# Four graph layers on one core: lots in one pair of PSUM banks, sums of propagations kept in three, similarity passes over two chunks

## The reference

```python
h = jnp.maximum(_layernorm(x, axis=-1), 0.0)
# layer 0
Wh = h @ W + b
sim = dot(Wh[row], Wh[col]) / max(|Wh[row]| * |Wh[col]|, 1e-8)
base = adj_v * softplus(deg_coeff[0] * deg_v + deg_coeff[1]) * (row != col)
prop_pos = segment_sum((base * relu(sim))[:, None] * Wh[col], row)
prop_neg = segment_sum((base * -relu(-sim))[:, None] * Wh[col], row)
x = x + scale * (coeff[0] * prop_pos + coeff[1] * prop_neg + coeff[2] * Wh)
# layers 1 to 3: sums over the same edges (counts, relu messages, sigmoid-gated messages)
```

## Time and profile before

| | us |
|---|---|
| median of 3 runs | 1847.92 (1847.14 to 1849.7) |
| the profiled execution, whole | 1844.67 |
| its span, first to last instruction | 1843.0 |
| `build`, blocks (first one-hot to last add) | 329.4 to 1184.2 |
| PE busy | 1153.8 (63%) |
| DVE busy | 1161.9 (63%) |
| ACT busy | 458.6 (25%) |
| mean granted clock of PE | 0.794 |

### The profile page before, as it was taken

The page is one execution under the profiler, slowest core; times in us unless marked ns, Lnnn a source line. Parts: engine busy times, 40 slices in busy tenths (PEclk is TensorE's granted clock), DMA queues, the critical chain, the costliest instruction groups (busy, mean ns, idle before and its releaser), DMA issues. The chain is left out here.

```text
span 1843.0 us, 38373 instructions
## 1 busy us (share of the span) xinstructions
PE 1153.8 (63%) x16508; PEld 977.7 (53%) x16508; DVE 1161.9 (63%) x2153; ACT 458.6 (25%) x1133; POOL 125.3 (7%) x215
## 2 busy tenths in 40 slices
PE   0000231677777877777787777547564767589997
PEld 0000121465655655655565556447564766389997
DVE  4860314888888888888888888659696442422222
ACT  1000101544444444444444444100000000012221
POOL 0710005200000000000000000000000000000000
PEclk9999956777778777777777777569786978579999
DMA  7316012121121121121121211164000000055552
GB/s 181 89 31 46 2 36 56 56 91 73 55 109 55 56 109 55 55 109 55 78 87 55 95 69 55 56 279 168 1 2 1 2 1 3 2 213 198 201 211 89
DMA packets 40247, 146.66 MB, mean 80 GB/s; under 512 B 24156, under 2 KB 24700, under 8 KB 33276
## 3 DMA queue, kind: packets, MB, share of 16 engines
q1 hardware_dynamic: 36252, 135.03, 20.9%
q0 software_dynamic: 2912, 7.92, 1.6%
q10 hardware_dynamic: 896, 1.04, 0.3%
HBM read 80.27 MB, written 63.72 MB: 78 GB/s over the span
## 5 line engine op out<-in xcount | busy, mean ns | idle before, releaser
L1065 PE MATMUL b_ps<-b_u_b,b_y 128*128 128x64 f32 x1250 | 207.8, 317 | 112.1 <-DVE k_xs L1028 106.5
L1065 PEld LDWEIGHTS b_ps<-b_u_b,b_y 128*128 128x128 f32 x1250 | 192.4, 233 | 131.5 <-DVE b_y L1022 128.5
L1232 PE MATMUL gcn_ps<-c_u,c_c 128*128 128x192 bf16 x1875 | 160.6, 250 | 117.2 <-PEq L85 77.3
L1065 PE MATMUL b_ps<-b_mv,b_soh 64*128 64x50 bf16 (+1 forms) x9600 | 221.1, 206 | 18.4 <-DVE b_mv L1006 12.9
L1232 PEld LDWEIGHTS gcn_ps<-c_u,c_c 128*128 128x128 bf16 x1875 | 159.3, 100 | 118.4 <-issue 77.8
L1065 PEld LDWEIGHTS b_ps<-b_mv,b_soh 64*128 64x128 bf16 x9600 | 196.1, 107 | 42.4 <-DVE b_mv L1006 13.9
L927 ACT ACTIVATE b_c_row<-b_ps 128x300 bf16<-128x300 f32 (+1 forms) x275 | 115.4, 420 | 408.6 <-PE b_ps L1065 407.3
L1006 DVE TENSOR_TENSOR b_mv<-b_mv,b_two 128x468 bf16<-128x468 bf16 (+1 forms) x600 | 179.5, 367 | 0.0
L1111 PEld LDWEIGHTS b_ps<-k_ident,b_a_row 128*128 128x128 f32 x625 | 81.3, 165 | 150.9 <-issue 93.6
L1111 PE MATMUL b_ps<-k_ident,b_a_row 128*128 128x128 f32 x625 | 129.5, 335 | 49.4 <-DVE b_scale L1014 49.4
L1014 DVE SCALAR_TENSOR_TENSOR b_scale<-head_rn_row,head_cap,b_ps 128x512 f32<-128x512 f32 (+1 forms) x175 | 120.3, 687 | 60.4 <-PE b_ps L1111 59.7
(11 more groups left out here) (224 smaller groups left out, 1080.7 us busy)
## 6 DMA issues: line engine op xcount, KB each, us to landing
g_blocks<-b_g_row SPq DMA_DIRECT2D x25, 1600.0 KB, 7.5
gated_row<-g_blocks SPq DMA_DIRECT2D x25, 1600.0 KB, 6.9
c_blocks<-b_c_row SPq DMA_DIRECT2D x25, 800.0 KB, 3.3
c_c<-c_blocks SPq DMA_DIRECT2D x5, 4000.0 KB, 32.1
edges_attr<-in_edge_attr SPq DMA_DIRECT2D x1, 5642.0 KB
head_rn_row<-rn SPq DMA_DIRECT2D x1, 1600.0 KB
rec<-sort_rec SPq DMA_DIRECT2D x1, 1209.0 KB, 4.9
k_xs<-in_x SPq DMA_DIRECT2D x1, 768.0 KB
```

Source lines behind the costliest of these rows:

```text
L1065: return nc.tensor.matmul(out, lhsT, rhs, start=start, stop=True, skip_group_check=True)
L1232: return nc.tensor.matmul(out, lhsT, rhs, start=start, stop=True, skip_group_check=True)
```

## The change

The eight PSUM banks are given out anew: lots have banks 0 and 1 alone, the similarities 2 and 3, AT is bank 4, and banks 5 to 7 (`SUM`) keep the propagations of 24 of the 25 column blocks through all 25 steps, with matmuls that add up in the bank. The 25th column block goes to AT[0:64] and is still added by DVE once in a step. The other adds are replaced by three at the very end (`folded`). `pos`, `sim` and `y` are made for two chunks at once (1024 columns, 4 groups `NG` in place of 7 chunks); `scale` and the transposes stay by chunk. The one-hots are split in two parts, "hi" and "hot", and both tables of order are new. A lot now waits for the copies of the lot just before it (`3 * i + 6` in place of `3 * i + 3`). The tiles `rel`, `qt` and `rest` of the head share the memory of `y`, and twelve small matmuls with zeros open the three sum banks.

```diff
-ORDER = [("lot", 0), ("lot", 1), ("chunk", 0), ("lot", 2), ("lot", 3), ("chunk", 1), ("prop", 0), ("lot", 4), ("chunk", 2),
...
+ORDER = [("lot", 0), ("chunk", 0), ("lot", 1), ("chunk", 1), ("lot", 2), ("prop", 0), ("lot", 3), ("prop", 1), ("chunk", 2),
+         ("lot", 4), ("chunk", 3), ("lot", 5), ("prop", 2), ("lot", 6), ("prop", 3), ("chunk", 4), ("lot", 7), ("chunk", 5),
+         ("lot", 8), ("lot", 9), ("chunk", 6), ("prop", 4), ("lot", 10), ("prop", 5), ("prop", 6)]
+VORDER = [("hi", 1), ("hot", 1), ("scale", 0), ("sim", 0), ("scale", 1), ("hi", 2), ("y", 0), ("hot", 2),
+          ("scale", 2), ("sim", 1), ("scale", 3), ("hi", 3), ("y", 1), ("hot", 3),
+          ("scale", 4), ("sim", 2), ("scale", 5), ("hi", 0), ("y", 2), ("scale", 6), ("sim", 3), ("y", 3), ("hot", 0), ("add", 0)]
...
-        SIM, AT, PR = 4, 6, 7
+        SIM, AT, SUM = 2, 4, 5
...
-            def positive(v, i):
...
+            def positive(v, g):
+                act.wait_ge(s["sims"], NG * v + (NG + g + 1))
+                nc.scalar.activation(side(pos, g), both(g), ACT.Relu, scale=coef[:, 0:1]).then_inc(s["pos"], 1)
...
-            def weigh(v, b, i):
...
+            def scaling(v, b, i):
...
+                dve.wait_ge(s["at"], NC * v + (2 * NC + i + 1))
+                nc.vector.scalar_tensor_tensor(scale[g % 2][:, lo:lo + n], rn_row[:, P * h0:P * h0 + n], cap[:, bass.ds(b, 1)],
+                                               ps[:, AT, 0:n], ALU.min, ALU.mult).then_inc(s["scaled"], 1)
+
+            def similar(v, g):
+                dve.wait_ge(s["made"], NG * v + (g + 1))
+                dve.wait_ge(s["pos"], NG * v + (g + 1))
+                nc.vector.scalar_tensor_tensor(side(sim[g % 2], g), both(g), coef[:, 1:2], side(pos, g),
                                                ALU.mult, ALU.add).then_inc(s["sgn"], 1)
...
-            def add(v, i):
-                h0, nh = CHUNKS[i]
-                dve.wait_ge(s["propped"], NC * v + (2 * NC + i + 2))
-                part = prop[:, h0:h0 + nh, :]
-                nc.vector.tensor_tensor(part, part, ps[:, PR, 0:nh * F].rearrange("p (h f) -> p h f", f=F),
-                                        ALU.add).then_inc(s["added"], 1)
...
+            def add(v):
+                dve.wait_ge(s["propped"], NC * v + (3 * NC + 1))
+                nc.vector.tensor_tensor(prop[:, NB - 1, :], prop[:, NB - 1, :], ps[:, AT, 0:F], ALU.add).then_inc(s["added"], 1)
...
+                for q in range(3):
+                    part = prop[:, 8 * q:8 * q + 8, :]
+                    nc.vector.tensor_tensor(part, part, ps[:, SUM + q, :].rearrange("p (h f) -> p h f", f=F), ALU.add).then_inc(s["folded"], 1)
...
+                for q in range(3):
+                    for j in range(4):
+                        mm(ps[:, SUM + q, P * j:P * j + P], k["zeros16"][:, 0:P], k["zeros16"][:, 0:P], j == 0)
...
-                pe.wait_ge(s["evac"], 3 * NL * w + (3 * i + 3))
+                pe.wait_ge(s["evac"], 3 * NL * w + (3 * i + 6))
...
-                            ins = mm(ps[:, 2 * pair + h, to:to + NB * (f1 - f0)], soh[b][rows, at, :], mv[b][rows, at, f0:f1, 0:NB],
+                            ins = mm(ps[:, h, to:to + NB * (f1 - f0)], soh[b][rows, at, :], mv[b][rows, at, f0:f1, 0:NB],
...
-                    pe.wait_ge(s["sgn"], NC * v + (i + 1))
+                    pe.wait_ge(s["sgn"], NG * v + (g + 1))
...
+                    pe.wait_ge(s["added"], v + 1)
                     pe.wait_ge(s["evac"], 3 * NL * v + (3 * NL + 6))
...
-                pe.wait_ge(s["made"], NC * v + (i + 3))
-                pe.wait_ge(s["added"], NC * v + (i + 1))
+                g, lo = i // 2, 512 * (i % 2)
+                pe.wait_ge(s["made"], NG * v + (g + 3))
                 for j in range(nh):
-                    ins = mm(ps[:, PR, F * j:F * j + F], y[i % 2][:, P * j:P * j + P], u_b[par][:, :], True)
+                    h = h0 + j
+                    to = ps[:, SUM + h // 8, h % 8 * F:h % 8 * F + F] if h < NB - 1 else ps[:, AT, 0:F]
+                    ins = mm(to, y[g % 2][:, lo + P * j:lo + P * j + P], u_b[par][:, :], h == NB - 1)
```

More of the change, by code:

```diff
@@ L756, in build @@
         gate_at, zero16, zero = l.sb("gate_at", [P, 1]), l.sb("zero16", [P, 1], BF16), l.sb("zero", [P, 1])
[L757 removed]
+        pos = l.sb("pos", [P, 1024])
         begun = l.sb("begun", [P, 6])
[L759 to L760 removed]
+        sim, scale = [l.sb(f"sim{i}", [P, 1024]) for i in range(2)], [l.sb(f"scale{i}", [P, 1024]) for i in range(2)]
+        y = [l.sb(f"y{i}", [P, 1024]) for i in range(2)]
+        rel, qt, rest = y[0][:, 0:512], y[0][:, 512:1024], y[1][:, :].rearrange("p (a n) -> p a n", a=2)
         ps = l.ps("ps", [P, 8, 512])
         names = ("index turned split rounded doubled hot onehot lot evac sims pos sgn weights made at scaled propped added "
[L763 removed]
+                 "folded further gate")
         s = {n: l.sem(n) for n in names.split()}
@@ L767, in build @@
         block = l.block()
-        SIM, AT, PR = 4, 6, 7
+        SIM, AT, SUM = 2, 4, 5
+        wide = lambda g: P * sum(CHUNKS[i][1] for i in range(2 * g, min(2 * g + 2, NC)))
+        side = lambda tile, g: (tile[:, 0:1024].rearrange("p (a n) -> p a n", a=2) if wide(g) == 1024
+                                else tile[:, 0:wide(g)])
+        both = lambda g: ps[:, SIM:SIM + 2, :] if wide(g) == 1024 else ps[:, SIM, 0:wide(g)]
         again = lambda r: not isinstance(r, int)
@@ L884, in _, with end @@
             pool.wait_ge(s["gate"], 5)
-            plan(pool, head, first, step, lambda r: None, widen)
+            def end(r):
+                if again(r):
+                    add_out(r, NB - 1, 0)
+            plan(pool, head, first, step, end, widen)
         @block.sync
@@ L954, in step @@
                         evacuate(r, w, par, i)
-                    if what == "chunk":
-                        positive(w - 1, i)
+                    if what == "chunk" and i % 2 == 0:
+                        positive(w - 1, i // 2)
             def end(r):
-                for i in range(NC):
-                    positive(r * NB + (NB - 1), i)
+                for g in range(NG):
+                    positive(r * NB + (NB - 1), g)
             nc.scalar.activation(begun[:, 4:5], k["ones"][:, 0:1], ACT.Copy).then_inc(s["evac"], 6)
@@ new lines, in add, with weighing @@
+            def add(v):
+                dve.wait_ge(s["propped"], NC * v + (3 * NC + 1))
+                nc.vector.tensor_tensor(prop[:, NB - 1, :], prop[:, NB - 1, :], ps[:, AT, 0:F], ALU.add).then_inc(s["added"], 1)
+            def weighing(v, b, what, i):
+                if what == "scale":
+                    scaling(v, b, i)
+                if what == "sim":
+                    similar(v, i)
+                if what == "y":
+                    weigh(v, i)
+                if what == "add":
+                    add(v)
```

92 lines of the change are left out of this document (42 added, 50 removed).

## The result

| | before | after |
|---|---|---|
| median of 4 runs, us (lowest to highest) | 1848.35 (1847.14 to 1849.7) | 1951.44 (1946.04 to 1954.28) |
| ratio, 95% interval | 1 | 1.0554 (1.053 to 1.0578) |
| profiled execution, whole / span | 1844.67 / 1843.0 | 1954.28 / 1952.6 |
| PE, DVE, ACT busy | 1153.8, 1161.9, 458.6 | 1274.4, 1086.8, 452.7 |
| mean granted clock of PE | 0.794 | 0.753 |

The change costs 103 us; the prediction said 1853, and 1885 at most. DVE has 75 us less to do, as foreseen, and PE, with practically the same matmuls, is busy for 121 us more. The span grew by 109.6 us. The timelines divide that at the first lot, the first lot of step 1, the first `scale` behind the last lot and the last add: +8.0 up to the first lot, +10.5 in the first block, +85.0 in the 24 steps (898.4 us for 813.4, so 37.4 us a step for 33.9), +8.5 behind them (32.2 for 23.7), -2.4 in the rest.

The account below looks back on a forecast made before the run. DVE was taken as nearest to full, trading waits with PE. Steps of 33.6 us for 33.96 gave -9, the first block +10, the tail +4: +5 us, 1853 in the median, range 1800 to 1885.

Parts of the forecast that it names:

- DVE's load: DVE in a step: relieved of 3.0 us, own work 24.4 us; windows should show it busy 25 to 26.
- The walk on PE: PE's prop, lot, prop, similarities, transposes before the next `scale`: 4.3 us at upper clock, 7.7 at lower; DVE waits 1.3 and 2.5.
- The two idle pieces: PE stands before the props of chunks 0 and 2, waiting for `y`: 1.5 to 2 us each.
- The clock's price: Slow clock on the two chains after PE's idle pieces: 1.8 us each, raising a step from 29.8 to 33.4 us.
- The seventh `scale` and the small stops: DVE's other waits in a step: 0.9 us before the seventh `scale`, 0.7 for smaller stops.
- the last part: Work after the last lot: 27.5 us against 23.7, about +4 us (0 to +8); a pair costs 7.6 to 10.6.
- The ends: First block and work after the last lot: about +10 and +4 us.
- First lot of step 1: First block: lots wait for copies, so this lot begins near 357 instead of 347.07, +10 us (8 to 11).
- Rival 2: PE becomes the bound through idle-lowered clock: steps 34.6 to 36 us, whole 1898 (1877 to 1911); chance 0.13.
- Rival 1: Clock holds better in the steps: 31.0 to 32.2 us each, whole 1804 (1790 to 1820); chance 0.32.
- Rival 3: One pair of banks for lots costs nothing, first block no longer: -5 us, whole 1843; chance 0.05.
- Rival 4: Change does not bite, adds were hidden behind PE already: whole within 4 us of 1848; chance 0.05.

Follow-up runs that it names:

- e3: Changed kernel plus 24 zero-operand matmuls before each of props 0 and 2, order otherwise the same: 1800.47 us, ratio 0.9785 to the kernel before.
- e7: Changed kernel plus 24 zero-operand matmuls before prop 0 alone: 1870.34 us, ratio 1.0132 to the kernel before.
- e1: Changed kernel with chunks 2 and 4 (similarities and transposes) moved ahead of the previous pair's props: 1714.8 us, ratio 0.9325 to the kernel before.
- e4: Kernel before with all lots on one pair of banks, each waiting for the previous lot's copies: 1891.62 us, ratio 1.0315.
- e9: Changed kernel with chunks 2 and 4 ahead of props, chunk 6 ahead of lot 9, and DVE adding again instead of sums in banks: 1691.92 us.
- e8: Changed kernel unedited, executed once more for its profile: 1953.48 us.

## Why the prediction was wrong

- **DVE's load.** Busy for 25 to 26 us a step was forecast; it is 25.4. Wide passes take 1.277 and 1.218 us, against 1.225 in the earlier trace rows; `pos` takes 1.114 for an estimate of 1.15. The sum itself had 24.4, counted from start to start. That is 1.0 us a step too little, which the figure of 25 to 26 should have told me: its four terms leave out the one add (0.22), and a `scale` that a wait follows counts for 0.75, not 0.66.
- **The walk on PE.** The two idle pieces lie where they were said to (1.59 to 2.00 us, said 1.5 to 2), and the late chain is what DVE waits for. At the upper level the walk holds: 4.1 us for the two chains in e3, said 3.8; 1.45 for e7's filled chain, said 1.3. The fall of the clock was placed too early for half the chains: the prediction called itself wrong if the props behind the idle pieces lasted 1.0 us rather than 1.9, and in 17 of 32 the first one did take 1.10. But 31 of the 32 met the lower level before their end. A third slow stretch, which the walk does not have, stands at the head of every step: the first similarities took 1.99 us in all 16. e1 has it too, where DVE waits for transposes for 1.6 us a step in all, so it costs DVE little.
- **The clock's price: the step that failed.** The prediction says that "the slow stretch of rows 7 held a prop, a lot and similarities before the full clock came back, which is half of such a chain, and I take 1.8 for each of the two." The rows do not say that. The transposes behind them take 1.11 us where 0.66 is the upper level, so they are slow as well, and the next prop is slow in part. Timeline of PE of before, right behind the earlier trace rows:

```profile
673.30 1.42 PE L1065 MATMUL b_ps<-b_u_b,b_y 128*128 128x64 f32 x8
674.65 1.25 PE L1065 MATMUL b_ps<-b_mv,b_soh 64*128 64x75 bf16 x72
```

  Read to its end, that stretch costs 0.93 + 0.18 + 0.93 + 0.45 + 0.41 = 2.9 us, not 1.8, which would have given some 35.8 us a step. Measured are 7.05 - 4.42 = 2.6 for a chain on the mean. DVE waited 149.0 / 16 = 9.3 us for the two, 5.5 above the 3.8 of the upper clock, where I had 3.6; the bound was 6.8. Fillers gave 5.8 back. In the step shown, where both chains are slow throughout, it waited 4.94 and 6.04 us where 3.1 and 4.3 were forecast.
- **Smaller terms.** The seventh `scale` and the small stops: (168.0 - 149.0) / 16 + 1.4 = 2.6 us, for 1.8. With 25.4 for 24.4 and 9.3 for 7.4 this makes 37.3 in place of 33.6. The clock's price is thus the largest of three errors of one sign: 1.9 us a step, beside 1.0 for DVE's work and 0.8 for the small terms. Together they are 3.7 x 24 = 89 of the 98 us that the forecast missed by; the last part has 4.5 more.
- **The ends.** First lot of step 1: 24.4 us behind the first lot, said 357 - 333.16 = 24; right. The last part: +8.5 for +4 (0 to +8), for the same reason, as both its chains ran at the lower clock. A pair took 11.0 and 10.8 us, said 7.6 to 10.6 (the terms given there make 10.8). Timeline of DVE of after there:

```profile
1274.98 0.75 DVE L1021 SCALAR_TENSOR_TENSOR b_scale<-head_rn_row,head_cap,b_ps 128x512 f32<-128x512 f32 x1 [6.89 <-PE b_ps L1140]
...
1285.82 0.75 DVE L1021 SCALAR_TENSOR_TENSOR b_scale<-head_rn_row,head_cap,b_ps 128x512 f32<-128x512 f32 x1 [6.89 <-PE b_ps L1140]
```

- **The rivals.** The upper bound of 37 us a step occurred, and the range of 1800 to 1885 didn't reach the 1935 that it means. Rival 2 had the right sign and the right loop (a late chain, an idle PE, a low clock), but stopped at 36 us a step, and gave it 0.13. Rival 1 needs a clock that holds; e3 and e1 are that case. Rival 3 is refuted for the kernel before by e4; there what the Trainium skill ("TensorE: Matmul & The Clock Gate", section on HAM oscillation) reports of one kernel of its own, that double-buffering in PSUM gave no further gain, does not carry over: taking the second pair away costs 54 us. What the Trainium skill says on the same page, in its section on psum-queue depth-cycling, that the clock falls and rises again with short stops between groups of matmuls, this trace bears out at both idle pieces (31 of 32 chains), though the stops here are waits for `y`. Rival 4 is wrong for the change, and right in a sense for one part of it (e9).

Open: why the clock falls ahead of the first prop in one chain and behind it in another (steps of after take 34.3 to 39.0 us); what one pair of banks costs within a step of the new order; and what the additions are worth with two pairs of banks for the lots. None of these was tried.

## What to carry to other kernels

Where an engine whose clock falls when it idles waits for another engine directly ahead of work that this one needs back, price that work at or near the lower clock throughout (here 2.6 of the possible 3.4 us on the mean), unless rows show otherwise. When rows are to say how long a slow stretch lasts, read on until a row takes its full-clock time again. Look in the in-order queue for work that needs nothing of the result waited for, and put it ahead of the wait: two entries of a table were worth 237 us here (227 by the ratios). What additions taken off an engine are worth (5 us in one order, 37 in another) can be said only with the waits around it.

## What the runs showed of the hardware

- 32 idle pieces of 1.59 to 2.00 us in 16 steps of after were followed in 31 cases by rows at the lower level, at once or behind the first prop (the prop took 1.97 us, or 1.10 and the similarities behind it 2.08); from 709.41 on the lower level held for 8.9 us. In e1 and e7, pieces of 0.18 and 0.26 us in the same place were followed by rows at the upper level.
- Matmuls with a zero operand in the idle piece kept the clock up, as similarities and transposes did there in e1: 24 of them in 1.51 us, and the next prop takes 1.10 us, for 1.97 in the step of after shown above.
- In the profiled execution of after, ACT and DVE stood for some 15 us at 305 to 320 us, beside nine of POOL's gathers that ran on (so not all engines stood, as the expectation of e8 has it), released by something that the profile calls remote. Neither e8 nor before shows it.

```profile
320.39 1.02 ACT L920 ACTIVATE b_fld<-b_ps 128x1024 bf16<-128x1024 f32 x1 [15.30 <-remote]
320.46 0.69 DVE L989 TENSOR_TENSOR b_y<-b_ps,head_dbase 128x512 f32<-128x512 f32 x1 [16.46 <-remote]
```
